# Summing and turning the gathered expert numbers: GpSimd and VectorE, or TensorE with the identity

## The reference, cut to what matters

```python
s1, i1 = top_k(sim1, 8)              # 32 keys a side, 8 heads, two sides
s2, i2 = top_k(sim2, 8)
all_idx = i1[..., :, None] * 32 + i2[..., None, :]
all_sc = s1[..., :, None] + s2[..., None, :]
fs, pk = top_k(all_sc, 8)
fi = take_along_axis(all_idx, pk)    # the expert numbers, 64 a token
hidden = gelu(xn . expert_down[fi]) * relu(fs)
out = sum(hidden * expert_up[fi])
```

## Time and profile before

| | |
|---|---|
| median of 3 runs | 1856.55 us (1856.44 to 1857.17) |
| the profiled execution | 1853.35 us, its span 1851.6 us |
| VectorE busy | 1554.3 us, 84% of the span |
| TensorE busy | 1331.8 us, 72% |
| ScalarE busy | 891.2 us, 48% |
| GpSimd busy | 732.0 us, 40% |
| mean granted TensorE clock | 0.819 of full speed |

### The profile page before, as it was taken

One profiled execution on the slowest core, in us unless ns is written; L12 is line 12 of the kernel. 1 busy time (PEld: TensorE's weight loads), 2 busy tenths in 40 slices (PEclk: granted clock), 3 DMA queues, 4 the chain that ended last, 5 costly groups with the idle time before them and its releaser, 6 DMA issues. The chain is left out here.

```text
span 1851.6 us, 53652 instructions
## 1 busy us (share of the span) xinstructions
PE 1331.8 (72%) x19632; PEld 922.5 (50%) x19632; DVE 1554.3 (84%) x7082; ACT 891.2 (48%) x1518; POOL 732.0 (40%) x1088
## 2 busy tenths in 40 slices
PE   3557687685877768597776959678685867868646
PEld 2333364563555455455544636455463645546436
DVE  2148999888998888889888898988889898898995
ACT  1656645445554544555454455545455554554110
POOL 1125363433445343344434344442444434353230
PEclk9778789796978969697896969879697987979665
DMA  2000000000000000000000000000000000000000
GB/s 74 1 7 8 7 10 7 15 7 15 8 1 16 7 15 7 15 8 1 16 7 15 8 7 10 7 16 7 15 8 2 15 7 16 1 14 2 8 1 14
DMA packets 30049, 19.61 MB, mean 11 GB/s; under 512 B 1824, under 2 KB 29216, under 8 KB 29728
## 3 DMA queue, kind: packets, MB, share of 16 engines
q1 hardware_dynamic: 29728, 15.23, 3.0%
HBM read 11.04 MB, written 4.19 MB: 8 GB/s over the span
## 5 line engine op out<-in xcount | busy, mean ns | idle before, releaser
L579 ACT ACTIVATE prob<-S 128x512 f32<-128x512 f32 x640 | 368.7, 599 | 436.2 <-PE S L749 270.1
L841 PE MATMUL G<-whot,onehot 128*128 128x16 bf16 x12288 | 379.3, 172 | 59.2 <-DVE hid L1233 24.3
L841 PEld LDWEIGHTS G<-whot,onehot 128*128 128x128 bf16 x12288 | 365.2, 100 | 91.9 <-issue 37.4
L1195 DVE TENSOR_TENSOR onehot<-lo_no,esel 128x1024 bf16<-128x1024 uint16 x512 | 387.2, 811 | 0.1
L747 PE MATMUL S<-qT,kT_even 128*128 128x512 bf16 (+3 forms) x512 | 153.0, 329 | 146.0 <-issue 100.3
L416 POOL TENSOR_TENSOR qk_a<-qk_n,cosw 128x256 f32<-128x256 f32 x64 | 58.1, 908 | 470.4 <-DVE qk_n L1012 433.9
L462 POOL TENSOR_TENSOR gat<-gat,cande 128x1280 f16<-128x1280 f16 x64 | 151.5, 2367 | 212.1 <-DVE gat L1156 212.1
L699 PE MATMUL S<-ident_b,stack 128*128 128x128 bf16 x1024 | 100.0, 270 | 146.6 <-POOL stack L432 113.4
L749 PE MATMUL S<-causal,ident_b 128*128 128x128 bf16 x1024 | 205.4, 233 | 0.0
L699 PEld LDWEIGHTS S<-ident_b,stack 128*128 128x128 bf16 x1024 | 84.1, 124 | 185.8 <-POOL stack L432 138.2
L1136 DVE FIND_INDEX8 topi<-topv,sims 128x8 uint16<-128x32 f32 x1024 | 166.2, 187 | 0.3 <-issue 0.3
(11 more groups left out here) (139 smaller groups left out, 2578.3 us busy)
## 6 DMA issues: line engine op xcount, KB each, us to landing
xa<-in_L_attn_x SPq DMA_DIRECT2D x16, 256.0 KB, 2.7
xr<-in_L_attn_x SPq DMA_DIRECT2D x16, 256.0 KB, 3.4
out<-r SPq DMA_DIRECT2D x16, 256.0 KB, 2.4
onehot<-in_L_ffn_expert_down SPq DMA_DIRECT2D x1, 512.0 KB, 6.0
up<-in_L_ffn_expert_up SPq DMA_DIRECT2D x1, 512.0 KB, 7.1
onehot<-in_L_ffn_keys SPq DMA_DIRECT2D x1, 256.0 KB, 6.4
onehot<-in_L_attn_w_qkv SPq DMA_DIRECT2D x1, 192.0 KB, 4.8
onehot<-in_L_attn_w_proj SPq DMA_DIRECT2D x1, 64.0 KB, 4.7
```

Source lines behind the costliest of these rows:

```text
L579: act.activation(dst, src, ACT.Exp, scale=SCALE).then_inc(exp_done.sem, 1)
L841: last = nc.tensor.matmul(bank[:, 16 * i:16 * i + 16], onehot[:, pair, t, :], whot[:, t, w_part, :], start=(w_part == 0), stop=(w_part == 2))
L1195: dve.tensor_tensor(onehot[:, pair, t:t + 8, :].rearrange("p t (c i) -> p t c i", i=2), lo, e, ALU.is_equal)
```

## The change

GpSimd's add and VectorE's sum are gone. `gat` is stored with the candidate outermost, so that the 64 columns of one candidate lie together. For each tile TensorE makes 20 products, one for each candidate: the 128 x 64 piece of `gat` is the stationary operand, the 128 x 128 identity in bf16 the moving one, and all 20 accumulate into 64 rows and 128 columns of the bank "sel". That sums the candidates and turns the result at once. The four tiles are done in steps 12, 19, 26 and 31 of TensorE's 40; in step 34 only the two turns of `fsel` are left. `elo` has memory of its own.

```diff
-        gat = sb("gat", [P, 2, H, NCAND, TOPK], fp16)
+        gat = sb("gat", [P, 2, NCAND, H, TOPK], fp16)
-        esel = sb("esel", [P, NT, H * TOPK], fp32)
-        elo = esel[:, :, :].rearrange("p t k -> p (t k)").bitcast(u16).rearrange("p (a t c) -> p a t c", a=2, c=2)
+        elo = sb("elo", [P, 2, P, 2], u16)
...
-        gat_done = signal("gat_done", 2 * NT)
-        esel_done = signal("esel_done", NT)
+        gat_done = signal("gat_done", NT)
+        numbers_turned = signal("numbers_turned", NT)
...
+        NUMBER_STEPS = [12, 19, 26, 31]
         SELECTION_STEP = 34
...
# GpSimd, candidates(b, t)
+                if t >= 2:
+                    pool.wait_ge(gat_done.sem, gat_done.value(b, t - 1))
...
# GpSimd, gather(b, t)
-                pool.tensor_tensor(g, g, cande[:, t % 2].unsqueeze(3).to_broadcast([P, H, NCAND, TOPK]), ALU.mult)\
-                    .then_inc(gat_done.sem, 1)
-                pool.wait_ge(gat_done.sem, gat_done.value(b, 2 * t + 1))
-                pool.tensor_tensor(g[:, :, 0:10], g[:, :, 0:10], g[:, :, 10:20], ALU.add)\
+                pool.tensor_tensor(g, g, cande[:, t % 2].rearrange("p h c -> p c h").unsqueeze(3)
+                                   .to_broadcast([P, NCAND, H, TOPK]), ALU.mult)\
                     .then_inc(gat_done.sem, 1)
...
# TensorE
+            def turn_numbers(b, t):
+
+                rows = slice(t % 2 * 64, t % 2 * 64 + 64)
+                pe.wait_ge(gat_done.sem, gat_done.value(b, t + 1))
+                if t == 0:
+                    wait_f_empty(pe, b, "sel")
+                for c in range(NCAND):
+                    last = nc.tensor.matmul(bank_f("sel")[rows, t // 2 * P:(t // 2 + 1) * P], gat[:, t % 2, c].rearrange("p h k -> p (h k)"),
+                                            ident_b[:, :], start=(c == 0), stop=(c == NCAND - 1),
+                                            skip_group_check=True)
+                last.then_inc(numbers_turned.sem, 1)
+
             def transpose_selection(b):
                 bank = bank_f("sel")
-                pe.wait_ge(esel_done.sem, esel_done.value(b, NT))
-                wait_f_empty(pe, b, "sel")
+                pe.wait_ge(fsel_done.sem, fsel_done.value(b, NT))
                 for pair in range(2):
                     two = slice(2 * pair, 2 * pair + 2)
-                    nc.tensor.transpose(bank[:, pair * P:(pair + 1) * P],
-                                        esel[:, two, :].rearrange("p t k -> p (t k)"), ident[:, :])
...
+                    if late is not None and step in NUMBER_STEPS:
+                        turn_numbers(late, NUMBER_STEPS.index(step))
...
# VectorE, top_pairs(b, t)
+                if t >= 2:
+                    dve.wait_ge(numbers_turned.sem, numbers_turned.value(b, t - 1))
+                dims = [P, NCAND, H, TOPK]
+                dve.tensor_tensor(gat[:, t % 2], psel[:, t % 2].unsqueeze(1).to_broadcast(dims),
+                                  cand_no[:, :, :].unsqueeze(2).to_broadcast(dims), ALU.is_equal)\
                     .then_inc(hotc_done.sem, 1)
-
-            def selected(b, t):
-                dve.wait_ge(gat_done.sem, gat_done.value(b, 2 * t + 2))
-                dve.tensor_reduce(esel[:, t, :].rearrange("p (h k) -> p h k", h=H),
-                                  gat[:, t % 2, :, 0:10, :].rearrange("p h c k -> p h k c"), AX.X, ALU.add).then_inc(esel_done.sem, 1)
```

More of the change, by code:

```diff
@@ L133, in attention_then_peer_layer @@
         psel = sb("psel", [P, 2, H, TOPK], u16)
-        gat = sb("gat", [P, 2, H, NCAND, TOPK], fp16)
-        qk_r = gat[:, :, :, :, :].rearrange("p a h c k -> p (a h c k)").bitcast(fp32)[:, 0:512]\
+        gat = sb("gat", [P, 2, NCAND, H, TOPK], fp16)
+        qk_r = gat[:, :, :, :, :].rearrange("p a c h k -> p (a c h k)").bitcast(fp32)[:, 0:512]\
             .rearrange("p (s t h d) -> p s t h d", s=2, t=2, h=NH)
-        esel = sb("esel", [P, NT, H * TOPK], fp32)
-        elo = esel[:, :, :].rearrange("p t k -> p (t k)").bitcast(u16).rearrange("p (a t c) -> p a t c", a=2, c=2)
+        elo = sb("elo", [P, 2, P, 2], u16)
         ehi = sb("ehi", [P, 2, P, 2], u16)
@@ L1154, in top_pairs @@
                 dve.wait_ge(top2_done.sem, top2_done.value(b, t + 1))
-                dims = [P, H, NCAND, TOPK]
-                dve.tensor_tensor(gat[:, t % 2], psel[:, t % 2].unsqueeze(2).to_broadcast(dims),
-                                  cand_no[:, :, :].unsqueeze(1).to_broadcast(dims), ALU.is_equal)\
+                if t >= 2:
[3 more added lines that the diff above has]
+                                  cand_no[:, :, :].unsqueeze(2).to_broadcast(dims), ALU.is_equal)\
                     .then_inc(hotc_done.sem, 1)
-            def selected(b, t):
-                dve.wait_ge(gat_done.sem, gat_done.value(b, 2 * t + 2))
-                dve.tensor_reduce(esel[:, t, :].rearrange("p (h k) -> p h k", h=H),
-                                  gat[:, t % 2, :, 0:10, :].rearrange("p h c k -> p h k c"), AX.X, ALU.add).then_inc(esel_done.sem, 1)
             def decode(b):
@@ L1253, in iteration @@
                     top_pairs(late, 1)
-                    selected(late, 0)
                     top_keys(late, 3)
@@ L1261, in iteration @@
                     top_pairs(late, 2)
-                    selected(late, 1)
                 if older is not None:
@@ L1266, in iteration @@
                     top_pairs(late, 3)
-                    selected(late, 2)
                 if b is not None:
@@ L1271, in iteration @@
                     apply_weights(older, 6)
-                if late is not None:
-                    selected(late, 3)
                 if older is not None:
```

## The result

The changed kernel takes 1883.42 us (median of 4 runs, 1880.38 to 1885.01), the kernel before 1856.49 us beside it. The ratio is 1.0143 (95% interval 1.0125 to 1.016): 26.9 us slower. The direction was forecast; the size was not: 1904 us was predicted and 1887 was the lower end of the range, so a loss of 47.8 us was forecast and 26.9 us measured.

What follows compares the result with a forecast made beforehand. The circle through TensorE's 40 steps, not VectorE's sums, was taken to bound the kernel. Fourteen selections at 3.80 us gave 53.2 - 4.5 + 2.4 - 3.3 = +47.8 us, on 1856.55 us: 1904 us, range 1887 to 1924.

Steps and rivals of the forecast that it cites:

- The circle: TensorE's 40 steps, `decode`, VectorE's one-hots, TensorE's weights and the branch set the period, 108.5 us on average; VectorE's sums beside it.
- rival (b): VectorE is the bound after all, so its 64 sums and the waits ahead come back: 1755 us; chance 0.03.
- The seven waits of TensorE for `apply_weights`: Waits in steps 24 or 25 in six selections and step 21 in one, expected to vanish: -4.5 us in all.
- the price: Each tile's turn: 20 products at 0.055 us plus two shape changes at 0.09 us, 1.28 us, partly hidden in steps 12 and 31.
- 3.80 less 0.3: Added time per iteration: four turns less 0.22 us for two saved turns, 3.80 us, less some 0.3 given back.
- (a): Weight loads of the turns' products not hidden: a turn costs 2.46 us, the whole about +120 us, 1977; chance 0.11.
- (c): The products hide and nothing changes, chance 0.02; or a cheap 0.025 us a product, +18 us, 1875, chance 0.03.
- both ends: First selection about +2.4 us, as turns no longer wait for the sum; last selection -3.3 us, where VectorE sets the end.
- How the numbers follow: Closing step: +47.8 us added to the profiled execution (1901.1) and to the median, 1904 us; range 1887 to 1924.
- some 6 us either way: Allowance in the range for the half-clock stretch at the start of TensorE's steps, shifted by a new period.

Runs made afterwards that it cites:

- a_sums: The changed kernel with VectorE's 64 sums put back at their old places, into memory that nobody reads; 1881.98 us, ratio 1.0142 to the kernel before.
- a_pad96: The changed kernel with 96 semaphore increments ahead of TensorE's first wait, which shift its loop's code; 1888.1 us, ratio 1.0173 to the kernel before.
- a_skip64: The changed kernel with 64 instructions in a jumped-over branch ahead of TensorE's loop, never executed; 1882.56 us, ratio 1.0144 to the kernel before.
- b_skip80: The kernel before with 80 instructions in a jumped-over branch ahead of TensorE's loop, never executed; 1837.26 us, ratio 0.9881.
- b_skip160: The kernel before with 160 instructions in a jumped-over branch ahead of TensorE's loop, never executed; 1827.56 us, ratio 0.9838.
- b_order160: The kernel before with 160 never-executed instructions ahead of TensorE's loop and some of VectorE's one-hots moved behind the normalisation; 1832.69 us, ratio 0.9856.

## Why the prediction was wrong

**Right: what bounds.** The circle of TensorE's 40 steps, `decode`, one-hots, weights and branch was the right one. VectorE's 64 sums put back cost nothing (a_sums), and rival (b), VectorE as the bound, fell. The seven waits of TensorE for `apply_weights` in the loop, put at 4.5 us, are gone in the changed kernel as forecast.

**Right: the price.** The turns cost 1.18, 1.33, 1.31 and 0.37 us where 1.13, 1.28, 1.28 and 0.33 were forecast. At the same kind of place, 43.5 against 47.0 us from the first scores to `decode` (before, a_pad96), the difference is 3.5 us, and 3.80 less 0.3 was forecast. At the places without the pause it is 3.0 to 3.5 (42.0, 42.1 and 42.3 against 45.3 and 45.5; a_skip64 with 46.0 lies above that). There b_skip80 and b_skip160 wait for `apply_weights` in 14 places of the loop instead of 7, some 9.5 us instead of 4.5, so that more is given back. Over the whole, b_skip80 and the changed kernel have nearly the same branch and the same short pause; their medians are 46.2 us apart, against 47.8. The match is closer than the measurements allow to say: the intervals leave some 4 us either way, the two profiled executions are 40.9 apart, and with the waits just named the forecast's own sum would be some 5 us less for this pair. Rivals (a) and (c) fell with it. The load of 64 columns is hidden: 0.056 us a product, where rows of fp32 loads had 0.114. The Trainium skill (TensorEngine Tiling, section Restrictions) says that column tiling turns the fast load off. The trace does not contradict it: the loads' records (PEld) are 114 ns long here on average, against 100 for the 128-column ones of the weights. But under a 128-column product it costs nothing here.

**Right: both ends.** The first `decode` came 2.6 us later (2.4 forecast), and from the fifteenth to the last it took 4.3 us less (3.3 forecast). There the turns run at half clock, 2.3 us each, as forecast.

**The step that failed** is the last one, "How the numbers follow": the sum was set on the profiled execution as though the rest of the loop stayed what it was, and for the start of TensorE's steps "some 6 us either way" were allowed, where some 20 were gained by the new place of the loop's code. The first measured part of that is the pause in step 1. It stood in the trace of before (15.3 us in 14 waits, one in each of the 13 passes of the loop and a short one at the end) and was in no term. The change puts 80 products with their loads in place of two turns into the iteration ahead of TensorE's loop, 156 more instructions, and that moved the border out of the first steps: 0.95 us an iteration. Moved back by 96 instructions, it is there again (a_pad96). The second is the stretch at half clock, 2.5 us shorter an iteration. Together they make the 1.4 us of the period that were missing. The kernel before, shifted by 80 instructions and nothing else, shows both in one number: 1837.26 against 1856.95, 19.7 us, and a period 1.4 us shorter. The sum of 47.8 us held for a kernel before without the pause (46.2), and the measured loss is what is left of it after these 19.7. That three differences add up so is arithmetic; what supports the account is that 46.2 is near 47.8, and that the shifts bring the pause and take it away.

How much of the 19.7 us is the pause itself, and how much the clock, is worked out only roughly: b_skip80 gains 1.5 us from the first scores to `decode`, 0.9 of it the pause, which leaves 0.6 for 2.7 us less at half clock. That a long half clock comes from the pause is suggested by all rows of the table with a pause over 1 us (8.8 to 9.5 us, against 6.1 to 8.7 without), but b_order160 has 12.4 without one; so other waits than this one may do it as well; no run holds the pause and changes the clock alone.

## What to carry to other kernels

Taking work off the busiest engine is worth nothing by itself where that engine waits at the end of the stretch; put back the removed work alone, into memory that nobody reads, and the run tells it. In a loop that refetches its code, an edit also moves the code: compare two versions at several shifts of the loop before a difference of one per cent is put down to the edit, and try the shifts for their own sake. A price per instruction from a neighbouring row held within some 5% here; what went wrong was the silent term "all else stays".

## What the runs showed of the hardware that was not expected

TensorE's loop (some 2,550 recorded instructions a pass before, 2,700 in the changed kernel) starts each pass with 6.7 to 8.2 us on average without a product, and in some places of the code with a further pause of 0.9 to 2.0 us between two products in step 1, where 0.4 is usual. 80 or 160 instructions ahead of it that are never executed took the time from 1856.95 to 1837.3 and 1827.6 us, and 256 left it at 1857.5. The pause stands at a place of the code that comes again after 256 instructions, and ends 1.2 to 1.6 us behind the landing of a 16.4 KB packet of instructions.
